# A seventh looked-up table for every other pair of tiles in a DLRM tower kernel, and the last tile's layers between its transposes

## The reference

```python
dots = jnp.einsum('bnd,bmd->bnm', e, e)
z = dots[:, iu, ju]                       # 496 pairs, i < j
h = jnp.concatenate([z, dense_ctx], axis=1)
h = jnp.maximum(h @ W_top1 + b_top1, 0.0) # 512 -> 512
h = jnp.maximum(h @ W_top2 + b_top2, 0.0) # 512 -> 256
y = h @ W_top3                            # 256 -> 1
```

## Time and profile before

| what | value |
|---|---|
| median of 3 runs | 896.4 us (894.67 to 901.53) |
| the profiled execution's own time | 895.49 us |
| its span, first to last instruction | 893.7 us |
| mean granted TensorE clock | 0.845 of full |
| gathers (L296) | 419, of 952 ns each |
| lookups (L339) | 1536 matmuls, 48 lookups |

### The profile page before, as it was taken

One profiled execution on the slowest core, in us unless ns is written; L12 is line 12 of the kernel. 1 busy time (PEld: TensorE's weight loads), 2 busy tenths in 40 slices (PEclk: granted clock), 3 DMA queues, 4 the chain that ended last, 5 costly groups with the idle time before them and its releaser, 6 DMA issues.

```text
span 893.7 us, 24184 instructions
## 1 busy us (share of the span) xinstructions
PE 588.3 (66%) x11019; PEld 519.5 (58%) x11019; DVE 224.9 (25%) x578; ACT 205.5 (23%) x369; POOL 399.7 (45%) x426
## 2 busy tenths in 40 slices
PE   3557668385683847748487583876838568384797
PEld 2456557275572746737376473765727557274696
DVE  3344223123131231213222231222312313122122
ACT  4252303103040031301213022030310304003142
POOL 7563625526254362533626346262552625436210
PEclk9788969698796987969789697896969879698769
DMA  9962313313122231321313223131231312213110
GB/s 225 239 206 62 94 50 78 91 44 98 49 79 80 56 103 37 86 69 55 107 44 87 57 66 102 44 92 50 79 91 44 98 49 76 76 53 92 35 32 2
DMA packets 37459, 70.97 MB, mean 79 GB/s; under 512 B 10382, under 2 KB 23438, under 8 KB 37358
## 3 DMA queue, kind: packets, MB, share of 16 engines
q0 software_dynamic: 20112, 54.95, 21.9%
q1 hardware_dynamic: 17246, 14.48, 7.0%
HBM read 69.39 MB, written 0.01 MB: 78 GB/s over the span
## 4 chain that ended last, share of the span: by engine, by line
PE 54%; another core or an unknown queue 27%; issue 10%; ACT 6%; DVE 2%; ACTq 0%; DVEq 0%
PE look_ps L339 17%; PE quad_ps L359 15%; PE top_ps L421 6%; PE top_ps L408 5%; PE quad_ps L323 5%; PE turn_ps L323 4%; ACT turned L484 3%; PE top_ps L398 1%; ACT ahead L491 1%; ACT area L513 1%; PE quad_ps L378 1%; DVE small L665 1%; DVE one_hot L675 1%; ACT products L507 0%
## 5 line engine op out<-in xcount | busy, mean ns | idle before, releaser
L296 POOL DMA_INDIRECT rows<-in_tbl,row_ids x419 | 398.9, 952 | 457.4 <-PE turn_ps L323 160.2
L359 PE MATMUL quad_ps<-turned 128*32 128x31 f32 x7680 | 139.5, 205 | 216.4 <-ACT turned L484 149.8
L339 PE MATMUL look_ps<-one_hot,small 125*128 125x256 f32 (+1 forms) x1536 | 243.0, 304 | 51.4 <-issue 39.1
L359 PEld LDWEIGHTS quad_ps<-turned 128*32 128x32 f32 x7680 | 107.0, 116 | 254.3 <-ACT turned L484 154.7
L339 PEld LDWEIGHTS look_ps<-one_hot,small 125*128 125x128 f32 x1536 | 211.1, 203 | 64.1 <-issue 60.2
L675 DVE TENSOR_SCALAR one_hot<-ids_across,sub_row 125x256 fp32r<-125x256 int32 (+1 forms) x384 | 110.9, 362 | 149.6 <-PE look_ps L339 129.8
L491 ACT ACTIVATE ahead<-look_ps 128x512 f32<-128x512 f32 (+1 forms) x48 | 28.3, 590 | 269.2 <-PE look_ps L339 253.3
L484 ACT ACTIVATE turned<-turn_ps 128x512 f32<-128x512 f32 x57 | 34.7, 625 | 209.0 <-remote 104.6
L323 PE MATMUL turn_ps<-ident,rows 128*128 128x128 f32 x424 | 65.8, 284 | 23.3 <-DMA rows<-in_tbl,row_ids 13.3
L484 ACT ACTIVATE turned<-quad_ps 128x512 f32<-128x512 f32 x55 | 33.6, 627 | 185.6 <-remote 104.2
L408 PE MATMUL top_ps<-area,w_sb 128*128 128x128 f32 x488 | 65.1, 275 | 2.0 <-issue 1.2
(11 more groups left out here) (50 smaller groups left out, 153.8 us busy)
## 6 DMA issues: line engine op xcount, KB each, us to landing
rows<-in_tbl,row_ids POOLq DMA_INDIRECT x419
ids_across<-in_small_ids SPq DMA_DIRECT2D x45, 128.0 KB
landed<-in_tbl SPq DMA_DIRECT2D x6, 896.0 KB
w_sb<-in_W_top SPq DMA_DIRECT2D x4, 256.0 KB
landed<-in_tbl SPq DMA_DIRECT2D x6, 104.0 KB
w_sb<-in_W_top SPq DMA_DIRECT2D x1, 512.0 KB
area<-in_dense_ctx SPq DMA_DIRECT2D x16, 8.0 KB
row_ids<-in_ids SPq DMA_DIRECT2D x1, 240.0 KB
```

Source lines behind the costliest of these rows:

```text
L296: pool.indirect_dma_start(out=rows[:, n % PLACES, j, :], out_offset=None, in_=tables[f], in_offset=bass.IndirectOffsetOnAxis(ap=row_ids[:, ...
L339: last = pe.matmul(look_ps[:, c * width:(c + 1) * width], small[:, f, r, part, c * P:(c + 1) * P], one_hot[n % 2][:, r, 0:width], start=(r ...
L359: last = pe.matmul(gram_ps[q * FIELDS:(q + 1) * FIELDS, g // BANK_GROUPS, at:at + COLS], turned[:, c, s, :], turned[:, c, s, 0:COLS], star ...
```

## The change

- `ODD_FIELDS` gets a fourth field, so seven tables are in SBUF (slot 6 is new). Six are looked up for every tile (`ALWAYS`); the seventh only for tiles t with t % 4 in (1, 2), that is 1, 2, 5, 6, 9, 10, 13, 14 (`looked`). One lookup serves a pair of them, so steps 0, 4, 8 and 12 get one more lookup. In these tiles unit 0 has one field, not two. All others are gathered as before.
- The room for the table (16 KB per partition) comes from `dynamic_dma_scratch_size=2048` (the memory in which GpSimd keeps the descriptors of its DMAs), from one place of `rows` (`PLACES = 8`), from one of three id buffers (`IDS_RING = 2`) and from `b2_sb`, which moves into a free part of `area`.
- The seventh table is loaded after the six, and split in step 0: ACT after the step's first lookup, DVE after its first one-hot matrix, both through one PSUM bank, so that each of the four copies waits for the subtraction before it.
- In the last tile's `turn_all` the first layer of tile 14 stands after units 7 to 10 (`LAST_LAYER1_AFTER = 7`), and its second layer after unit 11 (`LAST_LAYER2_AFTER`), where it stood after portion 0 of the dot products. ACT keeps the first layer's result ahead of unit 12.

```diff
-ODD_FIELDS = [6, 8, 9]
+ODD_FIELDS = [6, 8, 9, 14]
...
+    ALWAYS = SMALL - 1
+    PAIRED = [list(range(f, min(f + 2, FIELDS))) for f in range(ALWAYS, FIELDS, 2)]
+    ODD_PAIRED = [list(range(f, min(f + 2, ALWAYS))) for f in range(EVENS, ALWAYS, 2)]
+    def looked(t):
+        return SMALL if t % 4 in (1, 2) else ALWAYS
...
-        UNITS += [(later, unit) for unit in PAIRED]
+        UNITS += [(later, [f for f in unit if f >= looked(later)]) for unit in PAIRED]
-    PLACES = 9
+    PLACES = 8
+    LAST_LAYER1_AFTER = 7
+    LAST_LAYER2_AFTER = 11
-    IDS_RING = 3
+    IDS_RING = 2
...
-            LOOKUPS += [(f, n, min(2, TILES - n)) for f in range(EVENS + (n == 1), SMALL)]
+            LOOKUPS += [(f, n, min(2, TILES - n)) for f in range(EVENS + (n == 1), looked(n))]
...
             load_ids(1)
-            load_ids(2)
             load_table(1)
             sp.dma_start(row_ids[:, 1:TILES, :], ids[:, 1:TILES, :]).then_inc(row_ids_in[1], 16)
+            load_ids(2)
             load_ids(3)
+            for i in range(2, ALWAYS):
+                load_table(i)
             load_ids(4)
-            for i in range(2, SMALL):
-                load_table(i)
+            load_table(SMALL - 1)
...
@@ turn_all @@
-                    if LAYER1_AFTER <= i < LAYER1_AFTER + M1:
-                        layer1(t - 1, i - LAYER1_AFTER)
+                    first = LAST_LAYER1_AFTER if t == TILES - 1 else LAYER1_AFTER
+                    if first <= i < first + M1:
+                        layer1(t - 1, i - first)
+                    if t == TILES - 1 and i == LAST_LAYER2_AFTER:
+                        layer2(t - 1)
...
-                    if t > 0 and k == 0:
+                    if 0 < t < TILES - 1 and k == 0:
                         layer2(t - 1)
...
@@ split_high, and split_low in the same way @@
-                    if n >= 2:
+                    if i == SMALL - 1:
+                        act.wait_ge(low_parts, n)
+                    elif n >= 2:
                         act.wait_ge(low_parts, n - 1)
-                    act.activation(high_ps[n % 2], small[...],
+                    act.activation(high_ps[1 if i == SMALL - 1 else n % 2], small[...],
...
@@ scalar, step loop @@
+                        if t == TILES - 1 and i == LAST_LAYER2_AFTER - 1:
+                            keep_hidden1(t - 1)
-                    keep_hidden1(t - 1)
+                    if t < TILES - 1:
+                        keep_hidden1(t - 1)
                 for n in range(FIRST[t], FIRST[t + 1] - 1):
                     keep_looked_up(n)
+                    if t == 0 and n == FIRST[0]:
+                        split_high(SMALL - 1)
...
-    nc = bacc.Bacc("TRN2", target_bir_lowering=False, num_devices=1)
+    nc = bacc.Bacc("TRN2", target_bir_lowering=False, num_devices=1, dynamic_dma_scratch_size=2048)
```

More of the change, by code:

```diff
@@ L57, in dlrm_tower @@
     EVENS = len(EVEN_FIELDS)
-    PAIRED = [list(range(f, min(f + 2, FIELDS))) for f in range(SMALL, FIELDS, 2)]
-    ODD_PAIRED = [list(range(f, min(f + 2, SMALL))) for f in range(EVENS, SMALL, 2)]
+    ALWAYS = SMALL - 1
[3 more added lines that the diff above has]
+        return SMALL if t % 4 in (1, 2) else ALWAYS
     UNITS = [(0, unit) for unit in PAIRED + ODD_PAIRED]
@@ L140, in dlrm_tower @@
         b1_sb = sbuf("b1_sb", [P, M1])
-        b2_sb = sbuf("b2_sb", [P, HIDDEN2])
         ident = sbuf("ident", [P, P])
@@ L163, in dlrm_tower @@
         weighted = area[:, 3 * FEATURES:3 * FEATURES + HIDDEN2]
+        b2_sb = area[:, 3 * FEATURES + HIDDEN2:4 * FEATURES]
         y_rows = area[0:TILES, 0:P]
@@ L276, in _ @@
             load_ids(5)
+            load_ids(6)
             for t in range(TILES):
@@ L352, in gram @@
                 if t == 0 and portion == PARTS // 2:
-                    pe.wait_ge(low_parts, SMALL * STEPS)
+                    pe.wait_ge(low_parts, ALWAYS * STEPS)
                 for g in range(portion * GPP, (portion + 1) * GPP):
@@ L499, in place @@
                     act.wait_ge(gram_done, t)
-                both = [(slice(0, EVENS), t % 2), (slice(EVENS, SMALL), 1 - t % 2)]
+                both = [(slice(0, EVENS), t % 2), (slice(EVENS, looked(t)), 1 - t % 2)]
                 for fs, half in both if t > 0 else both[:1]:
@@ L559, in split_high @@
                     n = i * STEPS + k
-                    if n >= 2:
+                    if i == SMALL - 1:
+                        act.wait_ge(low_parts, n)
+                    elif n >= 2:
                         act.wait_ge(low_parts, n - 1)
-                    act.activation(high_ps[n % 2], small[:, i, k * AT_ONCE:(k + 1) * AT_ONCE, 0, :],
+                    act.activation(high_ps[1 if i == SMALL - 1 else n % 2], small[:, i, k * AT_ONCE:(k + 1) * AT_ONCE, 0, :],
                                    ACT.Copy).then_inc(high_copied, 1)
@@ L574, in _ @@
             keep_looked_up(EVENS)
-            for i in range(len(SPLIT_AFTER), SMALL):
+            for i in range(len(SPLIT_AFTER), ALWAYS):
                 split_high(i)
@@ L664, in split_low @@
                     dve.wait_ge(high_copied, n + 1)
-                    dve.tensor_tensor(small[:, i, part, 1, :], landed[:, i, part, 1, :], high_ps[n % 2],
+                    dve.tensor_tensor(small[:, i, part, 1, :], landed[:, i, part, 1, :],
+                                      high_ps[1 if i == SMALL - 1 else n % 2],
                                              ALU.subtract).then_inc(low_parts, 1)
@@ L702, in _ @@
                         make_one_hot(n)
+                    if k == 0 and t == 0:
+                        split_low(SMALL - 1)
                     if k == 0 and t > 0:
```

## The result

The changed kernel takes 915.5 us (median of 4 runs, 914.69 to 917.04); the kernel before, run beside it, 898.0 us. The ratio is 1.019 with an interval of 1.017 to 1.022. The forecast was 897.5 us, 887 to 907, so 1.1 us above the 896.4 us known when it was made: next to no change. The measured time lies 8.5 us above the upper end of the range.

A forecast was written before the change was run, and what follows sets the result against it. No engine was full; PE's finished work was taken to be seen late during POOL's gather bursts. Terms -8.8 + 6.0 + 3.3 - 2.5 + 2.0 + 1.0 = +1.0 us gave 897.5 us, range 887 to 907.

The forecast's parts named there:

- Room for the table: Descriptor scratch cut to 2048 bytes: no term in the sum, only a 0.05 chance that POOL runs out of room.
- rival C: POOL runs out of room for descriptors, so gathers wait until earlier ones have landed: about 921 us, chance 0.05.
- Shorter bursts: Stages before the dot products: seven bursts of 15 gathers instead of 16, each releasing the stage 1.255 us earlier: -8.8 us.
- rival A: In turn_all the stall doesn't count gathers, so bursts with fewer gathers save nothing: 906.5 us, chance 0.17.
- The fourth lookup: Steps 4, 8 and 12: one lookup more, partly hidden, costs 2.0 us a step, +6.0 us for three.
- the floor under the portions: Portions with a turn take 3.95 us from turn to turn, so most added lookup work at places 4 to 7 hides.
- Rival B: The lookups are hidden at places 3 and 8 too, and the opening gives both bursts: 887.6 us, chance 0.17.
- Opening and step 0: The opening's first burst stops two gathers earlier, -2.5 us; step 0 has three lookups instead of two, +3.3 us.
- The ids: IDS_RING = 2 makes a lookup's ids wait for the one-hot matrix two before, about 8 us ahead of use: 0.
- The end: Last tile: the second layer stands ahead of unit 12, so all 256 dot products start later: +2.0 us.
- The clock: Steps that begin earlier do more of their work at 1.2 GHz and give back part of the gain: +1.0 us.

The follow-up runs named there:

- b_scratch2k_look: The kernel before with a descriptor scratch of 2048 bytes instead of the default, nothing else, run once more on a quick chip: 561.4 us.

## Why the prediction was wrong, step by step

- *Room for the table.* The step that failed. The part on what the change removes and adds has no term for the smaller scratch: I asked only whether gathers would run out of room (rival C), found that they would not, and put it at nothing. They don't: the bursts go at 1.25 us as before. What the runs showed is 0.26 us at the gathers for which POOL had waited, but for those behind a burst of 15. On the first chip they are on the path: once ahead of each burst (25.96 - 25.50 = 0.45 us per tile with the later release) and four times in each step (some 0.3 us each). Over 14 tiles 14 x 0.45 + 14 x 4 x 0.3 = 23 us, an estimate; the portions behind a turn, summed from the two traces, give 16.3 us for the second part. The profiled executions missed the sum by 19.6 - 1.0 = 18.6 us, and the other terms took back the rest. That this is the price on the first chip is argued from its trace; that the scratch alone lengthens the answer is shown, on the other chips. No run with the full scratch and the rest of the change was made on the first.
- *Shorter bursts*, -8.8. Right in mechanism and size: about 1.4 us per burst (7 x 1.4 = 9.8), and rival A, that the count doesn't matter, falls. The gain was there and was spent by 14 x 0.45 = 6.3 us of lateness and 3 x 0.6 = 1.8 us of the fourth lookup.
- *The fourth lookup*, 2.0 us a step. On the first chip steps 4, 8 and 12 take 30.9 us (mean) and the other eleven 30.5: 0.4 us, because the floor under the portions rose with the longer answer and 16 matmuls fit below it. With the 0.6 us that place 8 costs ahead of the next burst it is 1.0 us, half of the forecast. Rival B was right about the places 4 to 7, on a floor that had become dearer. On a quick chip, without a floor, it is 3.5 us.
- *Opening and step 0*, +0.8; measured -1.25. The first lookup of step 0 starts 69.62 - 65.77 = 3.85 us earlier (2.5 forecast, 5.0 at most), and the step then takes 2.6 us longer (3.3 forecast).
- *The ids*, 0. Right on the first chip, where no wait for ids stands on the path, and wrong on the quick ones: I looked at what is queued behind the waiting ids, not at the weights ahead of them. A queue has to be read in both directions.
- *The end*, +2.0. Measured +2.5, by the forecast mechanism; the opposite on a quick chip.
- *The clock*, +1.0, for steps that begin earlier. Not seen as forecast: the stretch at 0.50 reaches 6.9 us into each step before; after, it reaches 5.6 to 8.6 us in, on average 6.9 us behind bursts of 15 and 7.2 us behind bursts of 16 (tile 14 left out, whose step has a second such stretch, longer after than before). The 3.6 us in the portions ahead of the first turn hold this spread and some of the fourth lookups; they can't be parted further.

The first lookup's row in the kernel after:

```profile
65.77 2.48 PE L352 MATMUL look_ps<-one_hot,small 125*128 125x256 f32 x10 [9.66 <-DVE small L688]
```

Open remain what makes PE's work be seen late on the first chip, what in the small scratch takes the 0.26 us and why the gather behind a burst of 15 is spared, and where between 2048 and 4096 bytes it begins.

## What to carry to other kernels

When a change pays for its room with a resource that isn't in the trace (a descriptor buffer, a ring, a place), price the latency of one use as well as whether it runs out: count how often an engine waits before using it, and ask for a small bound such as a few tenths of a microsecond each. Run the resource's reduction alone, and read one answer (releaser to released instruction) in two traces; it shows even where the time doesn't. And don't take a stall of one chip for a property of the kernel: here the same program is bound by late releases on the first chip, and by POOL's gathers or by PE on the six quick ones, and under the whole change the last tile grows by 2.5 us on the one and shrinks by 1.6 us or more (24.30 to 27.00 against 22.73) on the others.

## What was unexpected of the hardware

- The same kernel takes 897 us on the first chip and 559 to 563 us on six. Per middle tile (before against b_scratch2k_look, means) 13.5 us of the difference lie ahead of the dot products, with the late release in a burst of gathers (16.35 us against 0.64 us from unit 12's transposes to its copy), and 9.1 us in the step, where turns stand 4.0 us apart against 2.5 to 2.9. The granted clock is 0.845 against 0.99.
- `dynamic_dma_scratch_size=2048` puts 0.26 us more between the turn that POOL waits for and its gather (0.93 to 1.19, 0.87 to 1.13), on the first chip and on the quick ones where it ran; 4096 and 8192 don't. The gathers behind a burst of 15 are spared.
- Back to back a gather is issued every 1.25 us, in all traces and with every scratch.
